# Two more dense tile groups and a one-step last section in a two-layer graph kernel

## The reference

```
h = relu(layernorm(x))
# layer 0: a message is a row of one of two tables, by the edge's type
m = where(type == 0, h[src] @ W_data.T + b_data, h[src] @ W_control.T + b_control)
x = x + relu(segment_sum(m, dst) + h @ W_self.T + b_self)
h = relu(layernorm(x))
# layer 1: the weight of a message is made from a gate of both ends and the edge's own weight
g  = tanh((h @ gw_dst)[dst] + (h @ gw_src)[src] + gate_b)
yn = tanh(ew * yes + (1 - ew) * no)
e  = (g + yn) * 0.5 * d[dst] * d[src]          # d = degree ** -0.5
out = x + segment_sum(h[src] * e, dst)
```

## Time and profile before

| what | us |
|---|---|
| median of 3 runs | 5392.17 (5388.38 to 5398.95) |
| the profiled execution, its own time | 5411.43 |
| its span, first to last instruction | 5409.6 |
| layer 0: first gather of the main loop, last of it | 102.3, 2595.6 |
| layer 1: first gather of the main loop, last of it | 2849.6, 5219.3 |

### The profile page before, as it was taken

One profiled execution on the slowest core, in us unless ns is written; L12 is line 12 of the kernel. 1 busy time (PEld: TensorE's weight loads), 2 busy tenths in 40 slices (PEclk: granted clock), 3 DMA queues, 4 the chain that ended last, 5 costly groups with the idle time before them and its releaser, 6 DMA issues.

```text
span 5409.6 us, 123837 instructions
## 1 busy us (share of the span) xinstructions
PE 4380.4 (81%) x30900; PEld 3238.9 (60%) x30900; DVE 4470.6 (83%) x15813; ACT 3318.8 (61%) x11504; POOL 3928.9 (73%) x4029
## 2 busy tenths in 40 slices
PE   6588898988989899898467888888888878887864
PEld 4356666666666666665455666666666666665653
DVE  6888888878888888886467899898888988988973
ACT  5666777767777777775245566565656656665640
POOL 6777777767777677777727777777777777777774
PEclk9589999999999999999688999999999999999985
DMA  7777888778777787878555566565656665655544
GB/s 255 242 225 240 255 249 248 246 235 244 251 241 249 238 252 249 253 250 274 173 143 139 136 141 142 138 139 138 138 136 141 142 138 139 140 139 136 140 109 122
DMA packets 814769, 1028.32 MB, mean 190 GB/s; under 512 B 138839, under 2 KB 608379, under 8 KB 813563
## 3 DMA queue, kind: packets, MB, share of 16 engines
q1 hardware_dynamic: 677667, 752.38, 47.2%
q0 software_dynamic: 126976, 264.36, 20.0%
q10 hardware_dynamic: 9432, 3.66, 0.3%
HBM read 958.91 MB, written 60.97 MB: 189 GB/s over the span
## 4 chain that ended last, share of the span: by engine, by line
POOL 36%; issue 12%; PE 3%; DMA 3%; DVE 2%; SPq 0%; ACT 0%; DVEq 0%; POOLq 0%; ACTq 0%
POOL G L590 36%; PE PS L973 1%; DMA HTB<-t0s 1%; PE PS L961 1%; DMA NX<-t0s 1%; DMA HTB<-ini 1%; DMA OWF<-t0s 0%; DVE OHF L1217 0%; PE PS L924 0%; PE PS L1116 0%; DMA out<-OWF 0%; DVE ST L1206 0%; PE PS L992 0%; PE PS L933 0%; DMA OWF<-in_x 0%
## 5 line engine op out<-in xcount | busy, mean ns | idle before, releaser
L590 POOL DMA_INDIRECT G<-t,IDX x3760 | 3638.3, 968 | 1258.7 <-issue 1126.1
L730 ACT ACTIVATE OHF<-PS 128x384 bf16<-128x384 f32 x1960 | 960.6, 490 | 506.7 <-PE PS L961 476.4
L973 PE MATMUL PS<-CDST,OHF 128*128 128x256 bf16 x5880 | 975.1, 275 | 111.8 <-DVE CDST L1332 62.2
L822 ACT ACTIVATE ST<-PS,MV 128x1 f32<-128x1 f32 x1960 | 507.9, 259 | 562.8 <-DVE BB L1794 243.0
L1107 PE MATMUL PS<-HTB,NX 128*128 128x129 f32 x3920 | 821.6, 292 | 12.1 <-DVE NX L1780 11.0
L973 PEld LDWEIGHTS PS<-CDST,OHF 128*128 128x128 bf16 x5880 | 569.5, 99 | 432.5 <-ACT OHF L730 94.8
L1107 PEld LDWEIGHTS PS<-HTB,NX 128*128 128x128 f32 x3920 | 731.8, 197 | 157.9 <-issue 66.3
L841 ACT ACTIVATE OWF<-PS,ST 128x128 f32<-128x128 f32 x1960 | 700.6, 357 | 0.2
L1116 PE MATMUL PS<-CDST,OWF 128*128 128x256 f32 x1568 | 551.2, 435 | 174.7 <-ACT OWF L841 137.3
L833 ACT ACTIVATE ST<-ST,BASE 128x1 f32<-128x1 f32 x1960 | 558.6, 285 | 2.5
L1322 DVE TENSOR_SCALAR NX<-YN,PCODE 128x512 bf16<-128x512 int16 x980 | 324.4, 372 | 275.6 <-issue 145.9
(11 more groups left out here) (237 smaller groups left out, 8269.7 us busy)
## 6 DMA issues: line engine op xcount, KB each, us to landing
HTB<-t SPq DMA_DIRECT2D x980, 132.0 KB
HTB<-t0s SPq DMA_DIRECT2D x328, 384.0 KB
OWF<-t0s SPq DMA_DIRECT2D x326, 384.0 KB
NX<-t0s SPq DMA_DIRECT2D x326, 384.0 KB
YN<-rows SPq DMA_DIRECT2D x980, 64.0 KB
NX<-rows SPq DMA_DIRECT2D x980, 64.0 KB
G<-t,IDX POOLq DMA_INDIRECT x3760
t0s<-HTB SPq DMA_DIRECT2D x25, 384.0 KB, 3.5
```

Source lines behind the costliest of these rows:

```text
L590: eng.indirect_dma_start(out=G[:, k:k + width], out_offset=None, in_=table, in_offset=bass.IndirectOffsetOnAxis(ap=at, axis=0)).then_inc(s ...
L730: eng.activation(X0[:, k % KX, :, :].rearrange("p n w -> p (n w)"), PS[:, cell_bank(k), 0:384], ACT.Identity).then_inc(q_ev, 1)
L822: eng.activation(TH1[:, k % KW1:k % KW1 + 1], cell_slot(k)[:, D:D + 1], ACT.Tanh, bias=PDE[:, g % 2, b:b + 1]).then_inc(d_th, 1)
L973: ins = eng.matmul(PS[:, 4, 0:DW], X0[:, k % KX, n, :], CD0[:, k % KD, :], start=b == 0 and n == 0, stop=b == NB - 1 and n == 2)
```

## The change

The list of groups gets two groups of 60 tiles behind the twenty of 62: NG = 22, DT = 1360. TB falls from 104 to 8. By the formulas of the kernel SM becomes (3224 - 8 - 1360) / 8 = 232, NSB (the steps of a section) 1 instead of 13, NCT 170 instead of 155, and NSEC 403 instead of 31. A group spans 9 or 10 steps of layer 0, and LASTT becomes 214 instead of 216. To make room in YN for the longer codes, EWG and the first strip move to W2, whose weights are no longer used by then. The load of eight window starts is kept from reaching past the end of DS0.

```diff
-RUNS = ((20, 62),)
+RUNS = ((20, 62), (2, 60))
...
-TB = 104
+TB = 8
...
-        EWG = YN[:, HTE + 4 * GT:HTE + 5 * GT]
-        YG = YN[:, HTE + 5 * GT:HTE + 7 * GT].rearrange("p (g w) -> p g w", g=2)
-        HTE += 7 * GT
+        EWG = W2[:, D:D + GT]
+        YG = YN[:, HTE + 4 * GT:HTE + 6 * GT].rearrange("p (g w) -> p g w", g=2)
+        HTE += 6 * GT
...
-        STRIPS = [YN[:, HTE:HTE + D], OWF[:, 1792:1792 + D]]
+        STRIPS = [W2[:, 0:D], OWF[:, 1792:1792 + D]]
...
-                    q0 = q // 8 * 8
+                    q0 = min(q // 8 * 8, NQ - 8)
```

## The result

The changed kernel took **5449.0 us** (median of four runs, 5443.6 to 5454.6) beside 5392.0 for the kernel before: ratio 1.0106, interval 1.0091 to 1.0120, so 57 us slower. A second pair on another chip gave 5460.6 beside 5394.9: 1.0137, interval 1.0110 to 1.0164. The forecast was 5415, +23 us, in a range of 5365 to 5470. The sign and the range held; the size did not: the change cost two and a half times as much as forecast.

The account below looks back on a forecast made before the run. Layer 0 was taken as paced by dense work on PE and DVE, layer 1 by POOL's gathers. Terms -213 + 232 + 2 + 2 made +23 us, so 5415 us, range 5365 to 5470.

Parts of the forecast that it names:

- layer 1's term: Layer 1 main loop: fewer but fuller steps, DVE becomes the bound at 10.23 us a step; +2 us, upper bound +110.
- Twelve section steps less: Last sections of both layers: one step instead of 13, all before and after it stays; -213 us.
- Two more groups: Layer 0 main loop: the price is per group, two groups at 115.9 us; +232 us, bounds +207 and +264.
- the longer start: Start of layer 0: 120 more columns prepared and six more tiles placed; +2 us, bounds 0 and +12.
- The steps that go: Layer 0 main loop: 232 steps instead of 235 were taken at nothing, as groups of 10 steps are no shorter.
- Carrying the 19 us over: Whole kernel: the sum used the profiled 5411 us; the runs' median, 19 us lower, was assumed to keep that difference.
- Between the layers: Stretch after section 0 and before layer 1: forecast unchanged, 0 us.
- Rival 1: Layer 0: added cells fill PE's gaps, a group under 105 us; +183 for two groups, sum -26, 5366 us; chance 0.20.
- Rival 2: Layer 1: DVE paces it with its waits at 10.5 us a step; +65, sum +86, 5478 us; chance 0.13.
- Rival 3: Layer 0: denser steps cost 1.6 us more for each group; sum +55, 5447 us; chance 0.16.
- The flags: The fourth rival: flags trip for a new group, NPASS passes run and the time is a multiple; chance 0.01.
- The rule weighed: Layer 0: judged by weight loading, PE has a third to spare, so two groups would cost less than 232 us.

Follow-up runs that it names:

- f2: The changed kernel with 20 groups of 62 tiles, so the one-step last section alone; 5362.0 us, 0.9939 of the kernel before.
- f4: The changed kernel with layer 1's target one-hot comparison covering half of its columns, so layer 1's sums are not the reference's; 5405.3 us.
- f1: The changed kernel unedited, run again on another chip; 5460.6 us, 1.0137 of the kernel before.
- i1: The changed kernel with VectorE's two comparisons for the next four cells issued two cells later; 5252.4 us, 0.9726 of the kernel before.
- f3: The changed kernel with TB back at 104, so 22 groups with the 13-step section; 5601.8 us, 1.0386 of the kernel before.
- g3: The changed kernel without the third of the three matmuls of each layer 0 cell; 5424.1 us, 1.0039 of the kernel before.
- g2: The changed kernel with 20 groups of 64 tiles in place of more groups; 5262.7 us, 0.9739 of the kernel before.
- e1: The kernel before, unedited, on a chip where every kernel takes half as long again; 8097.6 us, ratio 1.0003.

## Why the prediction was right, and where it was wrong

The mechanism came as forecast in every part: group adds 116 us apart, one section step, and VectorE instead of POOL as the bound of layer 1. The size did not: +57 us for +23. **The step that failed is layer 1's term**, put at +2 us because VectorE's slack of 0.62 us a step was taken as wholly usable; it measured +17.8. The second, of nearly the same weight, is that the profile's 19 us over the median were carried over to the changed kernel, where only 6 showed.

- **Twelve section steps less: -213.** Right: -93.8 and -120.9 make -214.7.
- **Two more groups: +232.** Right in size: 115.6 us a group where 115.9 was taken. Layer 0 grew by 237.5, of which 7 lie before the first group add, where the forecast had put +2 for the longer start. The steps that go gave nothing back, as assumed. But it was a price read off without its cause. It holds only while VectorE stands before L1322 for 10% of the stretch; that row was in the trace of before (209.8 us of 2000) and I did not read it, since I read POOL, PE and the group adds there. It would not hold either where the gathers set the pace, as in layer 0 of f2.
- **Layer 1: +2. This is the mis-sized term; it measured +17.8.** I put DVE at 10.23 us a step and so 2373 us, against POOL's 2371 before. Both stretches are longer, since they have a start and an end: 2397 after, 24 over the forecast, and 2380 before, 9 over. The step explains the 15 us between the two gaps: DVE works through one of nine cells in 10.07 us and one of ten in 10.84, 10.29 on average, 0.06 more than forecast in each of 232 steps. The work of a step was even a little less than forecast: DVE's busy time is 0.898 x 10.09 = 9.06 us a step before and 0.950 x 10.29 = 9.78 after, +0.72 for the +0.76 taken. It was the slack: of DVE's idle time 0.52 us a step went and not 0.62, since the wait for ACT before L1757, counted as free for use, grew from 21.5 to 35.5 us. Why it grew, no run shows. The mechanism was right: the wait before L1747 went, POOL waits for PE, and f4 shows VectorE as the bound.
- **Carrying the 19 us over.** I added the sum to the median although the profile of before lay 19 us above it. The changed kernel's profiled run lay 6 us above its own, so 14 of the 57 us never were in the difference of the two profiles. The second profile of before is 9 us shorter in span. The sum of the parts by the means of two profiles is +46; against the medians (+57 and +66) 11 to 20 us stay unexplained. Single executions scatter by as much (5449 to 5473 in f1, whose profiled one was the fastest).
- **Between the layers: 0.** Measured +5.8 in the mean, in a part whose code is the same in all these kernels and whose length scatters by 13 us.
- **The rivals.** Rival 1 (gaps filled, under 105 us a group) did not happen, but was no fancy: i1 reaches 104.8 with no work taken away. Gaps fill when the order of VectorE's work lets them, not when cells are added. Rival 2 (10.5 us a step): layer 1 stayed at 2397 / 232 = 10.33, its start and end included; at 9.8 cells a step (f3) it was 10.63. Rival 3 (1.6 us more for each group) named 5447 us, and 5449 was measured, but that is a coincidence: the first 16 intervals are 115.6 and 115.9 us after, 115.9 and 115.0 before. The flags did not trip.
- **The rule weighed.** The Trainium skill, page "Perfetto Trace Analysis", section "Identifying the Most-Contended Engine", judges TensorE's headroom by weight loading, 64% in layer 0 before. That the two groups would therefore cost less than 232 us did not come true: they cost 230 between the first and the last group add. That PE alone was not the limit is what g3 shows, in which a fifth of the relief came back. Whether a third was to spare no run shows: in i1 a group is 8% cheaper, at 68% of weight loading (1369.61 of 2000) and 94% of matmul time.

The net effect of the change thus hangs on the order of VectorE's work: with the later comparisons, 22 groups end at 5252 us and 20 fuller groups at 5257, the same within the noise, where without them they are at 5461 and 5263. Whether the kernel before gains by the later comparisons on the common kind of chip was not measured, nor was which engine is next after i1.

## What to carry to other kernels

A price per unit read from the trace is good for a forecast of the same design, but only its cause tells what else could be had: when both full-looking engines lose work with little gain, look for the wait of an in-order engine that blocks both, and move the waiting instruction back before removing work. Size a relief or a load by the engine's busy time with overlaps counted once, not by durations times a count (g3: 7.3 us, not 27), and do not count every wait of an engine as room: some stay when it fills. A wait shown as "issue" before an instruction that reads loaded data deserves a comparison with the landing times. And where a unit of work can be filled further at no cost (64 tiles for 62), try that before adding units.

## What was not expected of the hardware

A 384 KB table block with its 64 KB of codes, the two issued 0.36 us apart by SyncE, landed 4.9 us after the block's issue (median in f1; one in ten over 5.9) at 240 GB/s in all. The same gather instruction cost POOL 1.284 us from start to start in layer 0 of g2 and 1.259 in its layer 1 (2780 to 5150 us), 2%, or some 49 us over 242 steps. And on two chips PE paused for 4 us about every 16 us (e1), with the same landings no later than elsewhere (4.0 us, at 155 GB/s in all); the cause stayed open.
